# Window attention: one broadcast transfer in place of repeated loads of the query stack

## The reference

```python
q = apply_rope(q) * d ** (-0.5)
k = apply_rope(k)
idx = q_pos + offsets                      # offsets -64 .. 0
local_mask = (idx < 0) | (idx >= S_k)
scores = jnp.einsum('bhqd,bhqwd->bhqw', q, k[:, :, gidx, :])
scores = jnp.where(mask, -jnp.inf, scores)
m = jnp.max(scores, axis=-1, keepdims=True)
e = jnp.exp(scores - m)
probs = e / jnp.sum(e, axis=-1, keepdims=True)
ctx = jnp.einsum('bhqw,bhqwd->bhqd', probs, v[:, :, gidx, :])
```

## Time and profile before

| | us |
|---|---|
| Median of three runs | 6191.22 |
| The three runs | 6180.91, 6191.68, 6191.22 |
| The profiled execution | 6180.91 |
| Its span, first to last instruction | 6179.1 |
| First scores of `window_attention` (PE, L778) | 491.62 |
| First scores of the last (64th) window | 988.55 |

### The profile page before, as it was taken

The page is one execution under the profiler, slowest core; times in us unless marked ns, Lnnn a source line. Parts: engine busy times, 40 slices in busy tenths (PEclk is TensorE's granted clock), DMA queues, the critical chain, the costliest instruction groups (busy, mean ns, idle before and its releaser), DMA issues. The chain is left out here.

```text
span 6179.1 us, 89337 instructions
## 1 busy us (share of the span) xinstructions
PE 5121.0 (83%) x27631; PEld 2709.8 (44%) x27632; DVE 3185.7 (52%) x6296; ACT 2505.7 (41%) x3173; POOL 1020.8 (17%) x786
## 2 busy tenths in 40 slices
PE   6778996689548999999999999999964089999970
PEld 3435554544214444444444444444343056666650
DVE  4555664311346888887888878888734000000013
ACT  1223442111113777776777667777620011111110
POOL 3440001401231000000000000000023700000016
PEclk8889998999777999999999999999976589999985
DMA  6445555710364343333333333333145421111115
GB/s 216 121 119 143 153 150 156 224 55 24 113 191 74 67 67 67 66 67 67 67 62 61 53 59 62 67 67 55 30 149 158 138 69 64 52 52 49 56 59 182
DMA packets 388644, 578.99 MB, mean 94 GB/s; under 512 B 90088, under 2 KB 284071, under 8 KB 386112
## 3 DMA queue, kind: packets, MB, share of 16 engines
q1 hardware_dynamic: 373536, 524.15, 35.5%
q0 software_dynamic: 14768, 50.51, 2.3%
HBM read 297.62 MB, written 197.24 MB: 80 GB/s over the span
## 5 line engine op out<-in xcount | busy, mean ns | idle before, releaser
L1153 DVE TENSOR_REDUCE full_peak<-full_item 128x1 f32<-128x512 f32 (+2 forms) x3392 | 2036.3, 655 | 462.1 <-PE full_item L1220 456.6
L1123 ACT ACTIVATE full_prob<-full_score 128x1024 f32<-128x1024 f32 (+1 forms) x1792 | 1651.2, 961 | 644.4 <-PE full_score L1231 636.1
L1220 PE MATMUL full_item<-full_kst,full_qst 49*128 49x512 f32 (+1 forms) x4096 | 1200.5, 405 | 45.1 <-DVE full_peak L1153 24.4
L1231 PE MATMUL full_score<-full_qst,full_kst 51*128 51x512 f32 (+1 forms) x3328 | 1107.1, 447 | 18.5 <-ACT full_prob L1123 13.1
L1245 PE MATMUL full_value<-full_prob,full_vaug 128*17 128x512 f32 x6656 | 887.3, 605 | 0.8 <-ACT full_raw L1110 0.7
L1231 PEld LDWEIGHTS full_score<-full_qst,full_kst 51*128 51x128 f32 (+1 forms) x3328 | 479.1, 183 | 931.5 <-ACT full_prob L1123 604.1
L1220 PEld LDWEIGHTS full_item<-full_kst,full_qst 49*128 49x128 f32 x4096 | 628.2, 188 | 189.3 <-DVE full_peak L1153 130.4
L2042 ACT ACTIVATE moe_hT<-moe_hbank,moe_b 128x512 f32<-128x512 f32 (+1 forms) x320 | 199.4, 623 | 807.4 <-PE moe_hbank L2097 803.0
L2109 PE MATMUL moe_ybank<-moe_w,moe_hT 128*128 128x256 f32 x2176 | 488.6, 386 | 5.2 <-ACT moe_hT L2042 5.2
L2097 PE MATMUL moe_hbank<-moe_xT,moe_w 128*128 128x512 f32 (+1 forms) x1280 | 476.2, 530 | 6.4 <-DMA moe_b<-in_b 6.4
L2109 PEld LDWEIGHTS moe_ybank<-moe_w,moe_hT 128*128 128x128 f32 x2176 | 417.2, 193 | 68.4 <-issue 6.0
(11 more groups left out here) (207 smaller groups left out, 5281.4 us busy)
## 6 DMA issues: line engine op xcount, KB each, us to landing
full_kst<-full_high SPq DMA_DIRECT2D x256, 200.1 KB
full_ctxT<-in_ctxT SPq DMA_DIRECT2D x16, 1601.0 KB, 9.3
full_kst<-full_low SPq DMA_DIRECT2D x128, 200.1 KB
win_qst<-scratch_q SPq DMA_DIRECT2D x384, 64.0 KB, 2.4
full_qst<-scratch_q SPq DMA_DIRECT2D x384, 64.0 KB
scratch_xbuf<-ctxp_zero POOLq DMA_DIRECT2D x17, 1024.0 KB
scratch_attn<-win_raw SPq DMA_DIRECT2D x64, 256.0 KB, 2.1
scratch_q<-open_parts SPq DMA_DIRECT2D x128, 128.0 KB, 2.3
```

What stands on the lines that cost most here:

```text
L1123: nc.scalar.activation(prob[h][(s.par * PAIRS + t) % 2][0:rows, 0:banks, :], score[u % 2][0:rows, 0:banks, :], ACT.Exp, scale=SCALE).then_ ...
L1153: nc.vector.tensor_reduce(peak[s.par][:, hq:hq + len(qts), c], src, AX, ALU.max).then_inc(item_read, 1)
L1220: ins = nc.tensor.matmul(ps[:, at:at + z - a], qst[s.slot][rows, h // 2, qt * P:(qt + 1) * P].bitcast(F32R), kst[s.slot][rows, h // 2, a:z ...
L1231: ins = nc.tensor.matmul(score[u % 2][0:z - a, kt % 2, :], kst[s.slot][rows, h // 2, a:z].bitcast(F32R), qst[s.slot][rows, h // 2, :].bitc ...
```

## The change

The six transfers of 16 rows for `qst` become three, of 48, 32 and 16 rows. The first reads query part 0 three times over (a step of zero in DRAM, three times 16 rows), the second part 1 twice. The same bytes are written to the same rows. `STACK_DMAS` falls from 10 to 7.

```diff
-        STACK_DMAS = 3 + 6 + 1
+        STACK_DMAS = 3 + 3 + 1
...
                 for part, times in ((0, 3), (1, 2), (2, 1)):
-                    for _ in range(times):
-                        sp.dma_start(q[at:at + HD, :, :].rearrange("r h k -> r (h k)"),
-                                     srq[part * HD:(part + 1) * HD]).then_inc(into, 16)
-                        at += HD
+                    rows = times * HD
+                    sp.dma_start(q[at:at + rows, :, :].rearrange("r h k -> r (h k)"),
+                                 srq[part * HD:(part + 1) * HD].unsqueeze(0).broadcast_to([times, HD, GROUP * SQ])).then_inc(into, 16)
+                    at += rows
```

## The result

The changed kernel takes 6390.63 us (median of three, 6389.06 to 6396.65), 1.033 times the kernel before (95% interval 1.0306 to 1.0353): slower by about 200 us where I had forecast about 100. The profiled spans are 6381.2 and 6179.1. The difference arises in `window_attention`. I take a window's start from PE's first L778 row of each window: first 502.1, last 1198.0, 11.05 us per window against 7.89, so 3.16 x 63 = 199 us, and 10.5 us at the stage's start; the stages behind it give some 7 us back.

The account below looks back on a forecast made before the run. PE's 7.32 us per window is the floor; a two-window circle through SP's load issue and the late shift sets 7.89. Circle +69, stage start +5, clock +27 make +101 on 6180.91: 6282 us, range 6235 to 6340 (eight of ten: 6235 to 6400).

Parts of the forecast that it names:

- The direction and its cause: Window stage: slower, chance 0.86, as the merged transfers run on 3 and 2 DMA engines, the second's among the first's.
- SP's saving: SP's load issue: q transfers take 1.9 us instead of 2.75, 0.85 us less per two windows.
- The circle: Loop over two windows, scores to store, next load, shift, scores: 15.94 us before, 18.2 after, +69 us over 63 windows.
- the sum from T to the scores: From a load's first transfer to the scores: keys and store, two pieces, remaining transfers, PE's start; 9.5 us instead of 7.26.
- T + 9.5: T is when a load's first transfer goes out; the scores waiting for its shift were to start 9.5 us later.
- The two pieces: The 48-row and 32-row q transfers: 65,536 bytes per engine each, 2.73 us each, one after the other, 5.46 us.
- the clock: TensorE at half clock after long waits: 1.7 us lost in every second circle, 27 us, bounds 0 and 54.
- the start of the stage: Three loads issued before the first shift: first scores at 497 instead of 491.62, +5 us.
- store to load: SP's time from the store to the next load's first transfer: 1.14 us in the circle.
- Sixteen engines: Rival: transfers use all 16 engines, or two or three suffice; 27 us faster, 6154 us; chance 0.07.
- different engines for the two pieces: Rival: 48-row and 32-row transfers land on different engines, so the effects cancel, around 6181 us; chance 0.06.
- The slow rate of 16.1 GB/s: Rival: the busiest engine is the bound, 11.7 us per window, up to 6430 us; chance of over 6340: 0.17.

Follow-up runs that it names:

- rows_outermost: Kernel after with the 16 rows as outer step and the repetition inside, for queries and keys: 6172.99 us, 0.9995 of the kernel before.
- the two halves of the change: Kernel before with only the 48-row transfer merged, 6296.16 us (1.0183), or only the 32-row one, 6304.44 us (1.0205).
- store_later: Kernel before, with SP storing window s-2 instead of s-1 in the body of s: 6142.15 us against 6179.42, 0.9935.
- q32_only: Only part 1 goes as one 32-row transfer, part 0 as three of 16 rows: 6304.44 us, 1.0205 of the kernel before.
- no_keys: Kernel after with the key stacks loaded once per buffer ahead of the stage: 6324.00 us, 1.0233 of the kernel before.
- no_values: Kernel after with the values loaded once per buffer ahead of the stage: 6373.41 us, 1.0314 of the kernel before.
- The filler: Kernel after with 26 more mask matmuls on PE before it waits for an even window's shift: 6334.31 us, 1.0263 of the kernel before.
- shift_act_after: Kernel after with the shift's transfer issued by ACT in a queue of its own: 6377.99 us, 1.0323 of the kernel before.

## Why the prediction was right or wrong

- **The direction and its cause** were right: a shift behind transfers that run on 3 and 2 engines, both on the same two. `rows_outermost` removes the cost with nothing but the order of dimensions; the shares of 0.19 and 0.13 show their number, the landings in the two halves of the change show that they are the same.
- **SP's saving** was half right: 2.18 us for the q part where I took 1.9, load to shift 4.3 on average instead of 4.86, 0.5 less and not 0.85. Nothing came of it.
- **The circle** was right, in the windows 10 to 55: load to scores + scores to store + store to load is 12.0 + 9.8 + 0.75 = 22.5 us, and the pair of windows is 9.5 + 13.0 = 22.5 from PE's starts. In the kernel before `store_later` gained 37 us, where the earlier trace rows showed 33 us of waits.
- **The first step that failed is the sum from T to the scores.** I had T + 9.5, it is T + 12.0. The two pieces were sized about right: the landing of the engine with one piece and the earlier one with two lie 2.84 us apart on average (2.89 between none and one in `q32_only`), 2.73 forecast; the distance is no clean measure of a piece, since it is 1.58 in `no_keys` and 2.33 in `no_values`. What I under-sized is the rest, 9.5 - 5.5 = 4.0 where it is 12.0 - 2 x 2.84 = 6.3: the keys by 0.7 and the values by 0.2 (`no_keys`, `no_values`); the busiest engine lands its last packet 0.8 us behind its neighbour, which has the same pieces, and I had treated the two as one. The other 0.6 us stays open. 2.5 / 2 x 63 = 79 us. One thing that the sum left out lies at the end of the queue: the next load is issued at 717.72, T + 7.7, before the shift has landed, and then nearly all engines are busy (row 718.80:720.60), at 211 / (0.90 x 16) = 14.7 GB/s each, where the sum took 24 for the third q transfer, the values and the shift. No run separates this from the rest.
- **The second is the clock.** I assumed one loss of 1.7 us in every second pair of windows, 27 us. The waits do not spread: they come as one of about 5.3 us in every pair (against 1 us before), and in nearly every pair PE ran at half clock for a while, scores to store 9.77 us instead of 7.55. The filler gives 59 us back. That is 32 us more than forecast; of my bounds of 0 and 54 the upper one was too low, because I had taken one loss in two pairs where it comes in nearly all, and the stretches at half clock are longer than the 3.41 us of the earlier trace rows: 6.8 us on average from 520 to 1100, 10.24 in the row 718.43:728.67.
- Smaller: the start of the stage 502.1 instead of 497, +5 us; store to load 0.75 to 0.95 instead of 1.14, some -9 us. 101 + 79 + 32 + 5 - 9 = 208, against 209 from the windows' starts and 202 in the spans. That it closes to 1 us is in part luck: 12.0 and 0.75 to 0.95 are averages over windows 10 to 55, whose mean window is 11.26 us and not 11.05.
- **The rivals.** Sixteen engines, and different engines for the two pieces, are ruled out by the shares and by the halves of the change. The slow rate of 16.1 GB/s is ruled out for the pieces, which ran at 25 to 26 GB/s, but not for the end of the queue (14.7 GB/s in the row 718.80:720.60). Nor is the busiest engine the bound: 188,416 bytes in 11.05 us are 17 GB/s, below the 25 that it reached. The price of this rival (up to 250 us) was nearer the result than its mechanism.

## What to carry to other kernels

Before merging transfers, look at the outermost step count of the merged one on both sides: a repetition put outside turns a transfer over 16 engines into one over 2 or 3; put inside, it cost nothing here (0.9995). Then look at what small and urgent transfer stands behind it, on its queue or on its engines: here a queue of its own gained nearly nothing (1.0323 against 1.0332), and storing one window later only a third of the loss (1.022). Count the waits of TensorE by their length as well as by their sum, since those of 5 us here cost a third more in half clock.

## What the runs showed of the hardware that I had not expected

- A transfer in the same dimensions with the 16 rows outermost and the repetition inside keeps 16 engines: in the trace a load's seven transfers bring 114 updates of their semaphore (7 x 16 is 112), where the kernel after has 87 (5 x 16 + 3 + 2 is 85). The stage's DMA share was 0.51 against 0.37.
- SP needs about 0.37 us to issue a transfer of whole rows, and 0.57 to 0.80 us for most with a third dimension, zero step or not (median 0.568 for the q transfers of `rows_outermost`, 0.674 for those of the kernel after, 0.800 for its shift). The third dimension alone does not decide it: the values' transfer, 128 by 4 by 64, takes 0.400. Merging two plain transfers into one of the dearer ones saves next to nothing on SP.
- Two queues that meet on an engine can alternate packet by packet though their packets differ in size: 0.17 us per 256-byte packet of the shift beside the load's 4096-byte packets, in `shift_act_after`.
- Adding 26 matmuls per pair of windows made the kernel 0.7% faster (1.0332 to 1.0263), by the clock alone (1.00 against 0.85 in the middle of the stage).
